# Scores of a 16-head attention: from block-diagonal keys over 128 rows to strips of 32 rows

## The reference

```python
def _L2_xattn_ref(q, k, v, mask, Wq, bq, Wk, bk, Wv, bv, Wo, bo):
    B, S, D, H = (2, 256, 128, 16); DH = D // H          # 16 heads of 8 features
    def proj(x, W, bias):
        return (x @ W + bias).reshape(b, -1, H, DH).transpose(0, 2, 1, 3)
    qh, kh, vh = proj(q, Wq, bq), proj(k, Wk, bk), proj(v, Wv, bv)
    scores = jnp.einsum('bhqd,bhkd->bhqk', qh, kh) / math.sqrt(DH)
    scores = jnp.where(mask, -jnp.inf, scores)
    attn = jax.nn.softmax(scores, axis=-1)
    out = jnp.einsum('bhqk,bhkd->bhqd', attn, vh)
    return out.transpose(0, 2, 1, 3).reshape(b, -1, D) @ Wo + bo
...
x = x + _L2_xattn_ref(_layernorm(x), ctx_1024, ctx_1024, mask, ...)
x = x + _L2_ffn_ref(_layernorm(x), ...)
x = x + _L3_xattn_ref(_layernorm(x), ctx_1024, ctx_1024, ...)   # the same, without a mask
x = x + _L3_ffn_ref(_layernorm(x), ...)
```

## Time and profile before

| | |
|---|---|
| median of 3 runs | 573.1 us (572.79 to 574.89) |
| span of the profiled execution | 569.1 us |
| PE busy | 441.2 us (78% of the span) |
| PE weight loads busy | 377.0 us (66%) |
| DVE busy | 354.7 us (62%) |
| ACT busy | 247.8 us (44%) |
| POOL busy | 178.2 us (31%) |
| chain that ended last | PE 64%, DVE 19%, ACT 4%, issue 4%, others 9% |
| scores (L1047) on that chain | 7% of the span |

### The profile page before, as it was taken

How to read it: one execution, slowest core, us unless ns; L and a number is a source line. 1 busy time by engine, 2 the same in 40 slices (tenths; PEclk the granted TensorE clock), 3 DMA queues, 4 the chain that set the end, 5 groups by cost and what they waited for, 6 DMA issues and landing times.

```text
span 569.1 us, 7825 instructions
## 1 busy us (share of the span) xinstructions
PE 441.2 (78%) x2586; PEld 377.0 (66%) x2587; DVE 354.7 (62%) x777; ACT 247.8 (44%) x466; POOL 178.2 (31%) x220
## 2 busy tenths in 40 slices
PE   2979999999999968899895799774257998492015
PEld 2868988999999956799784489772135988340005
DVE  2747787777777764433658566246766650648982
ACT  2557667767767634333212254312503542034110
POOL 4230051231200002696173466217434340105300
PEclk9989999999999996899958999665559995666557
DMA  8740000000000019100000000000000000000001
GB/s 183 233 112 1 1 1 2 0 0 0 0 0 0 1 14 69 8 1 0 0 1 0 2 0 2 1 0 0 1 0 1 1 0 1 1 1 0 0 0 37
DMA packets 28156, 9.62 MB, mean 17 GB/s; under 512 B 17855, under 2 KB 26849, under 8 KB 28129
## 3 DMA queue, kind: packets, MB, share of 16 engines
q1 hardware_dynamic: 26876, 8.66, 9.8%
q10 hardware_dynamic: 1253, 0.61, 0.4%
HBM read 8.74 MB, written 0.52 MB: 16 GB/s over the span
## 4 chain that ended last, share of the span: by engine, by line
PE 64%; DVE 19%; ACT 4%; issue 4%; SPq 3%; DMA 3%; POOL 2%; DVEq 0%; ACTq 0%; POOLq 0%
PE bank L1047 7%; PE bank L1082 6%; PE bank L827 5%; PE bank L457 5%; PE bank L459 5%; PE bank L458 5%; PE bank L816 4%; PE bank L962 4%; PE bank L817 4%; PE bank L1061 3%; PE bank L848 2%; SPq L512 2%; PE bank L1198 2%; PE bank L925 2%; PE bank L1078 2%
## 5 line engine op out<-in xcount | busy, mean ns | idle before, releaser
L1572 DVE TENSOR_TENSOR probT_lo<-bank,probT_hi 128x512 fp32r<-128x512 f32 (+1 forms) x80 | 55.1, 689 | 24.9 <-ACT probT_hi L1280 24.2
L1280 ACT ACTIVATE probT_hi<-bank 128x512 fp32r<-128x512 f32 (+1 forms) x80 | 47.6, 595 | 41.1 <-PE bank L827 41.0
L1565 DVE TENSOR_REDUCE neg_max<-bank 128x1 f32<-128x589 f32 x64 | 49.2, 768 | 19.2 <-PE bank L817 17.9
L596 POOL TENSOR_TENSOR rstd<-var_eps,minus_half 128x4 f32<-128x4 f32 x14 | 14.8, 1060 | 133.2 <-DVE var_eps L1506 133.2
L1271 ACT ACTIVATE shared<-bank,neg_max 128x589 f32<-128x589 f32 x64 | 48.0, 750 | 5.7 <-DVE neg_max L1565 5.6
L672 POOL TENSOR_TENSOR scratch<-scratch,neg_max 128x1232 f32<-128x1232 f32 x16 | 36.0, 2248 | 43.1 <-DVE neg_max L1841 43.1
L827 PE MATMUL bank<-ident,shared 128*128 128x128 f32 (+1 forms) x320 | 48.0, 272 | 0.1
L1047 PE MATMUL bank<-k_blocks,queries 128*128 128x308 f32 x128 | 38.5, 446 | 7.7 <-ACT queries L1377 3.3
L1024 PE MATMUL bank<-ident,pmax 128*1 128x128 f32 x7 | 2.2, 344 | 53.0 <-DVE pmax L1602 53.0
L827 PEld LDWEIGHTS bank<-ident,shared 128*128 128x128 f32 (+1 forms) x320 | 39.8, 142 | 2.6 <-ACT shared L1271 0.4
L1047 PEld LDWEIGHTS bank<-k_blocks,queries 128*128 128x128 f32 x128 | 24.1, 199 | 21.1 <-issue 11.8
(11 more groups left out here) (340 smaller groups left out, 1205.0 us busy)
## 6 DMA issues: line engine op xcount, KB each, us to landing
shared<-in_mask_Bx16xSxS_bk SPq DMA_DIRECT2D x8, 154.0 KB, 7.9
shared<-in_L_xattn_Wkv SPq DMA_DIRECT2D x4, 256.0 KB, 7.3
w<-in_L_ffn_W SPq DMA_DIRECT2D x1, 1024.0 KB
shared<-in_L_xattn_Wq SPq DMA_DIRECT2D x2, 256.0 KB, 5.5
x_residual<-in_x ACTq DMA_DIRECT2D x2, 256.0 KB, 6.7
shared<-in_L_xattn_Wo SPq DMA_DIRECT2D x2, 256.0 KB, 9.0
out_x<-x_residual SPq DMA_DIRECT2D x1, 512.0 KB, 3.2
bo<-in_L_xattn_bo SPq DMA_DIRECT2D x3, 64.0 KB, 3.8
```

The source lines that it names most:

```text
L1280: nc.scalar.activation(probT[HI][0:n, SLOT[c], :], bank[0:n, PT_BANK[b][c], :], ACT.Copy)\
L1565: nc.vector.tensor_reduce(neg_max[:, b, i:i + 1], scores0(i), AX.X, ALU.max, negate=True)\
L1572: nc.vector.tensor_tensor(probT[LO][0:n, SLOT[c], :], bank[0:n, PT_BANK[b][c], :], probT[HI][0:n, SLOT[c], :].bitcast(F32), ALU.subtract). ...
```

## The change

Scores are computed in strips: a matmul takes 32 rows only, the four heads that lie in them, and with four strips all 16 heads. In a strip the keys are compact: `k_quad` has 4 x 77 columns for all 128 rows, and in column block j only those rows are kept whose head is the j-th of its strip (`quad_of_row`, which is made from `head_of_row` once, near the start). Every strip writes the same bank as its four heads did before. The banks, the columns and what DVE reads from them stay as they are.

Keys and queries are split into a high part and a rest of type fp32r, and each strip has three matmuls (high x high, high x rest, rest x high) that accumulate, where an fp32 matmul goes through the array four times. The order is pass by pass, the four strips inside. POOL makes the two parts of the keys, with three instructions over 308 columns for one over 1232. ACT writes the high part of the queries, DVE a rest by a new instruction; the pair of buffers `qT` is that of the first attention. The scale by the root of the head's size moves from the queries to the keys. `queries_of(1)` moves ahead of `scores(0)`.

The diff, with few lines around what changes:

```diff
         bo16 = sb("bo16", [P, 2, D])
-        bq16 = sb("bq16", [P, 2])
+        bk16 = sb("bk16", [P, 2])
         head_of_row = sb("head_of_row", [P, HM])
+        quad_pair = sb("quad_pair", [P, 2, 4])
+        quad_of_row = sb("quad_of_row", [P, 4])
         half_of_row = sb("half_of_row", [P, 2])
...
         k16T = sb("k16T", [P, 2, B, NC])
-        k_blocks = sb("k_blocks", [P, B, HM, NC])
+        k_quad = sb("k_quad", [P, 4, NC])
+        k_blocks = [sb(f"k_blocks_{n}", [P, B, 4, NC], F32R) for n in ("hi", "lo")]
         v_pair = sb("v_pair", [P, 2, B, D])
...
                 own.settle()
+            own.add(nc.gpsimd.tensor_tensor(quad_pair[:], head_of_row[:, 0:8].rearrange("p (g j) -> p g j", g=2),
+                                            head_of_row[:, 8:16].rearrange("p (g j) -> p g j", g=2), ALU.add))
+            own.settle()
+            own.add(nc.gpsimd.tensor_tensor(quad_of_row[:], quad_pair[:, 0, :], quad_pair[:, 1, :], ALU.add))
+            own.settle()
             pool.wait_ge(cT_ok, 2)
...
                 for b in range(B):
-                    nc.gpsimd.tensor_tensor(k_blocks[:, b], k16T[:, n, b, :].unsqueeze(1).to_broadcast([P, HM, NC]),
-                                            head_of_row[:].unsqueeze(2).to_broadcast([P, HM, NC]), ALU.mult)\
+                    own.add(nc.gpsimd.tensor_tensor(k_quad[:], k16T[:, n, b, :].unsqueeze(1).to_broadcast([P, 4, NC]),
+                                                    quad_of_row[:].unsqueeze(2).to_broadcast([P, 4, NC]), ALU.mult))
+                    own.settle()
+                    own.add(nc.gpsimd.tensor_copy(k_blocks[HI][:, b], k_quad[:]))
+                    own.settle()
+                    own.add(nc.gpsimd.tensor_tensor(k_blocks[LO][:, b], k_quad[:], k_blocks[HI][:, b].bitcast(F32),
+                                                    ALU.subtract))
+                    own.settle()
+                    nc.gpsimd.tensor_copy(va_pair[:, n, b, :, :, DH], half_of_row[:].unsqueeze(1).to_broadcast([P, NPAIR, 2]))\
                         .then_inc(kv16_spread, 1)
-                    half = half_of_row[:].unsqueeze(1)
                     by_pair = v_pair[:, n, b, :].rearrange("p (c h d) -> p c h d", c=NPAIR, h=2)
...
                                                 half_of_row[:, hd:hd + 1], None, ALU.mult).then_inc(kv16_spread, 1)
-                    nc.gpsimd.tensor_copy(va_pair[:, n, b, :, :, DH], half.to_broadcast([P, NPAIR, 2]))\
-                        .then_inc(kv16_spread, 1)
                     by_head = v_left[:, n, b, :].rearrange("p (h d) -> p h d", h=HM)
...
                     pe.wait_ge(q16_ok, B * n + b + 1)
-                    q = q16T[:, b, (t % TPB) * P:(t % TPB + 1) * P]
                     if t:
                         pe.wait_ge(s16_taken, m)
-                    for g in range(4):
-                        last = nc.tensor.matmul(bank[:, g, 0:BK * NC], q,
-                                                k_blocks[:, b, BK * g:BK * (g + 1), :].rearrange("p h k -> p (h k)"),
-                                                start=True, stop=True)
+                    for stationary, moving in ((HI, HI), (HI, LO), (LO, HI)):
+                        begin, end = stationary == moving, stationary == LO
+                        for g in range(4):
+                            rows = slice(32 * g, 32 * (g + 1))
+                            last = nc.tensor.matmul(bank[:, g, 0:BK * NC],
+                                                    qT[stationary][rows, b, (t % TPB) * P:(t % TPB + 1) * P],
+                                                    k_blocks[moving][rows, b].rearrange("p h k -> p (h k)"),
+                                                    start=begin, stop=end)
                     last.then_inc(s16_in_psum, 1)
...
                 queries_of(0)
-                pe.wait_ge(kv16_spread, 8 * B * (n + 1))
+                queries_of(1)
+                pe.wait_ge(kv16_spread, 7 * B * (n + 1))
                 scores(0)
                 scores(1)
-                queries_of(1)
                 for t in range(NT + 1):
...
             for n in range(2):
-                row = vrow[f"L{n + 2}_xattn_bq"][0] - FIRST
-                nc.scalar.activation(bq16[:, n:n + 1], bank[:, 1, row:row + 1], ACT.Copy, scale=SC16)\
+                row = vrow[f"L{n + 2}_xattn_bk"][0] - FIRST
+                nc.scalar.activation(bk16[:, n:n + 1], bank[:, 1, row:row + 1], ACT.Copy, scale=SC16)\
                     .then_inc(vcol_ok, 1)
...
                 act.wait_ge(kv16_in_psum, n + 1)
-                row = vrow[f"L{n + 2}_xattn_bk"][0]
                 nc.scalar.activation(k16T[:, n], bank[:, 0, 0:B * NC].rearrange("p (b k) -> p b k", b=B), ACT.Identity,
-                                     bias=vec_cols[:, row:row + 1]).then_inc(kv16_ok, 1)
+                                     bias=bk16[:, n:n + 1], scale=SC16).then_inc(kv16_ok, 1)
                 nc.scalar.activation(v_pair[:, n], bank[:, 1, 0:B * D].rearrange("p (b d) -> p b d", b=B), ACT.Copy)\
...
                 norm_copy(k)
+                row_q = vrow[f"L{n + 2}_xattn_bq"][0]
                 for b in range(B):
                     act.wait_ge(q16_in_psum, B * n + b + 1)
-                    nc.scalar.activation(q16T[:, b, :], bank[:, 6 + b, :], ACT.Identity, bias=bq16[:, n:n + 1],
-                                         scale=SC16).then_inc(q16_ok, 1)
+                    nc.scalar.activation(qT[HI][:, b, :], bank[:, 6 + b, :], ACT.Identity,
+                                         bias=vec_cols[:, row_q:row_q + 1]).then_inc(q16_hi_ok, 1)
                 for t in range(NT + 1):
...
                 norm_copy(k)
+                row_q = vrow[f"L{n + 2}_xattn_bq"][0]
+                for b in range(B):
+                    dve.wait_ge(q16_hi_ok, B * n + b + 1)
+                    nc.vector.scalar_tensor_tensor(out=qT[LO][:, b, :], in0=bank[:, 6 + b, :],
+                                                   scalar=vec_cols[:, row_q:row_q + 1],
+                                                   in1=qT[HI][:, b, :].bitcast(F32), op0=ALU.add, op1=ALU.subtract)\
+                        .then_inc(q16_ok, 1)
                 if n == 0:
...
                 LAG = 3
```

More of the change, by code:

```diff
@@ L363, in build @@
         q16_in_psum = sem("q16_in_psum")
+        q16_hi_ok = sem("q16_hi_ok")
         q16_ok = sem("q16_ok")
```

## The result

The changed kernel takes 579.6 us (median of 4 runs, 578.8 to 581.0) where the kernel before takes 572.9 (median of 4). The quotient of the two medians is 1.0117; the comparison of the runs gives a ratio of 1.0132 with a 95% interval of 1.0105 to 1.016. It is 6.7 us slower; the profiled executions are 7.9 us apart, with spans of 577.0 and 569.1.

The account below looks back on a forecast made before the run. PE was taken to bound each turn of the stages. All ten open turns at the lower clock level cost 26.4 us, less 11.3 for four upper ones: 15.1 on 573.1 gives 588, range 564 to 612.

Parts of the forecast that it names:

- The price of the scores: A tile's twelve score matmuls on PE, in strips side by side, take 0.5 to 0.8 us; today 2.08.
- (b): Loads of the strips run one behind the other: twelve take 2.5 us, a turn 9.0; 610 us, chance 0.18.
- (c): Strips run in sequence: twelve take 3.1 us at the lower level, a turn 9.5; 615 us, chance 0.10.
- The price of a turn: One tile's turn on PE in a stage takes 4.8 us at the upper clock level, 7.63 at the lower.
- the clock falls: In both stages PE's clock falls to the lower level soon after the query matmuls; forecast chance 0.52.
- rival (a): The clock holds in at least nine of the ten open turns; all upper gains 7.1 us, 566, chance 0.20.
- the change of sign: Slower turns to faster at 9.3 upper turns of ten (26.4 / 2.83), named as at least nine.
- The rows that stood against (a): Earlier trace: clock fell after 8-row matmuls, stayed low under 77-row ones, rose by 298.6 under 128-row ones lasting 3.52 us.
- the number of turns at the upper level: Four of ten open turns, five per stage, get the upper level; each gives 2.83 us back, 11.3 together.
- The stretch to tile 1's transposes: From DVE's first addition or copy in each stage, 14.05 us today: averages at the lower level add 2.03.
- The second stage starts: With three passes DVE's first copy of scores can begin at about 426.6 instead of 428.56, a gain of 2.0 us.
- Keys and queries: POOL's key blocks stay about 2.2 us, hidden some 20 us ahead; the first stage's query steps gain 0.7.

Follow-up runs that it names:

- fill_full: The kernel with full filler: changed kernel plus unused 128-row matmuls behind the strips of tiles 2 to 7 and in the three turns without scores; 552.2 us.
- full_rows: Changed kernel with the split kept but strips taken back: twelve matmuls of 308 columns over all rows per tile; 578.7 us.
- strip_by_strip: Changed kernel with its loops over strips and passes exchanged, so the three matmuls of one strip follow each other; 579.4 us.
- the pair of fillers: Changed kernel with the same unused matmuls added at the same places, over 128 rows or only rows 96 to 127; 552.2 and 598.2 us.

## Why the prediction was right in sign and too high in size

It said slower, 588, range 564 to 612. It is slower, 579.6. The range holds faster and slower kernels alike, so lying in it says little; what was right is the sign and the reason for it. Of the 15.1 us of the sum, 9.9 are found in the stages, and 2.0 are given back outside them.

- The price of the scores held: 0.5 to 0.8 was taken. In the kernel with full filler they run from 341.93 to 342.56 at the upper level, 0.63; over all rows twelve such matmuls take 1.77 (453.24 to 455.01 in full_rows). That is 2.8 times; the Trainium skill (TensorE: Matmul & The Clock Gate, Packing small matmuls) has 3.07 for four strips, and the traces are near it. (Divided by it, 1.7 gives 0.55 and not the 0.56 of the prediction.) Rivals (b) and (c), loads or strips one behind the other, asked for 2.5 and 3.1 us at the lower level; there the twelve take 1.07. The 0.14 between passes and strip_by_strip say the same.
- The price of a turn held: 7.66 against 7.63, and 4.71 to 4.92 against 4.8.
- That the clock falls held, and that it is the reason is shown by the pair of fillers: with the same strips, 552.2 over 128 rows and 598.2 over 32. The term of rival (a), 7.1 gained if the level is held, came out near (7.4, in part by luck), but not its condition: the clock did not hold. Nine upper turns of ten, which the prediction named for the change of sign, would by its own sum still have lost 0.9 us (26.4 less 25.5).
- The rows that stood against (a), and the earlier trace rows, were thin evidence. The lower level of that place lasts from 285.0 to 298.6, and matmuls over 128 rows stand at its start too:

```profile
285.88 3.54 PE L1117 MATMUL bank<-kq,xnT 128*128 128x77 f32 x16
```

The clock did not rise behind these 3.54 us. That the rows of an operand matter here was shown only by the two fillers.
- The term that was mis-sized is the number of turns at the upper level. I took four of ten without a row that fixed it; there are about 5.1 (45.8 for six lower turns less 41.04 and 36.23, each by 2.83). That is 3.0 of the 5.2 us missing in the stages.
- The stretch to tile 1's transposes cost 1.6 and 0.9, not 2.0 each: 1.6 us. The averages in it are 4.29 in the first stage as predicted (330.40 to 334.69); the shorter scores take the rest out, which the text allowed for and left out of the sum.
- The second stage starts 2.6 earlier instead of 2.0: 0.6.
- Keys and queries held. POOL's three instructions are 0.70, 0.44 and 0.83 us, 2.2 with their waits, instead of 2.26. But the cover that I named for them, 20 us to the first scores (it is 21 in the first stage of the kernel before and 32 in the second), is the wrong one: full_rows shows that the roots of the layer norm queued behind them come first.
- The 2.0 us outside the stages were not forecast. Nothing there is changed but the preparation of the keys. The stretch behind the second stage has the same program in all kernels and takes 85.6 in before, 83.8 in after, 84.0 in fill_full, 85.4 in full_rows; in one of its windows of 15 us the granted clock is 0.77 before and 0.86 after. I take it for the clock falling at other places there; that was not tried.

## What to carry to other kernels

Before work is taken off TensorE, look at what the clock does where that work is already missing, such as the last turns of a pipeline: that showed here what most of the stage would become. In this kernel packing the scores into strips gained only together with unused matmuls over all rows, and 0.7 us of them in the right gap decided over several microseconds. For a step moved into another engine's queue, the cover is the next instruction in that queue that someone waits for, not the step's own reader.

## What the runs showed of the hardware that was not expected

- A TensorE without any gap for 42.40 us stayed at 1.2 GHz (granted clock 0.51), with its filler and its scores over 32 rows. That dense work can stay low for so long I had not expected. Not all of it had few rows: of a turn of 8.7 us there, 2.3 are transposes and 4.3 are averages, over 104 and 128 rows. So the rows decide between the two fillers, but they are not the whole of it, and what else counts is open.
- Matmuls of different strips overtake each other: in strip_by_strip the first passes of all four strips start at 318.51 to 318.55, ahead of the second passes of any (from 318.73 on), though the program has three strips' first passes behind the second pass of the first strip.
- A DVE instruction of 0.42 us takes 2.53 beside a POOL instruction of 2.26. The Trainium skill (SBUF — State Buffer, Who interferes with whom) says that a tensor_scalar on DVE can take a mode with two ports, in which it and POOL lock a shared pair against each other for a whole instruction. The trace agrees: the DVE instruction starts 0.01 us behind POOL's and ends 0.28 us behind its end.
